# Attention and routed FFN on one core: a clear ahead of every indirect DMA, and another order and bank plan for the tile loop

## The reference, cut to what matters

```
x: (4, 1024, 256)      context: (4, 77, 256)
x = x + attention(layernorm(x), context)       # 16 heads of 16, softmax over 77 keys
n = layernorm(x)                               # without scale and shift
scores = sigmoid(n @ gate.T)                   # 32 experts
choose 4 of 8 groups by their best score + bias, then 6 experts in them
w = chosen scores / their sum * 2.5
x = x + sum over the 6 experts of w_e * down_e(silu(gate_e n) * up_e n)
      + shared_down(silu(shared_gate n) * shared_up n)
```

## Time and profile before

| | |
|---|---|
| median of 3 runs | 870.69 us (869.93 to 871.14) |
| profiled execution, its own time | 878.87 us |
| its span | 877.2 us, mean granted TensorE clock 0.896 |
| busy share of the span | PE 88%, DVE 57%, ACT 45%, POOL 59% |
| chain that ended last, by engine | PE 39%, POOL 31%, issue 17% |
| indirect DMAs on POOL | 192 scatters, mean 986 ns; 192 gathers, mean 1025 ns |
| pauses on POOL | 160, mean 615 ns |

### The profile page before, as it was taken

The page is one execution under the profiler, slowest core; times in us unless marked ns, Lnnn a source line. Parts: engine busy times, 40 slices in busy tenths (PEclk is TensorE's granted clock), DMA queues, the critical chain, the costliest instruction groups (busy, mean ns, idle before and its releaser), DMA issues.

```text
span 877.2 us, 17678 instructions
## 1 busy us (share of the span) xinstructions
PE 768.9 (88%) x5472; PEld 658.4 (75%) x5472; DVE 500.7 (57%) x1556; ACT 393.0 (45%) x822; POOL 517.3 (59%) x603
## 2 busy tenths in 40 slices
PE   4699989988899999959997999999999999899920
PEld 2488877777777777624655999999999998799920
DVE  4667666666666667522345223367666665466652
ACT  1264444444444444210111566666666665466610
POOL 0204777777777777777000000778888887888885
PEclk9698888899988888678999899999999999899965
DMA  9113444444444322245513355888888898788852
GB/s 292 42 46 112 132 133 139 138 137 138 139 141 153 120 84 90 103 152 196 188 49 96 110 172 165 239 249 267 262 269 264 258 268 250 209 247 261 257 156 72
DMA packets 120222, 149.01 MB, mean 170 GB/s; under 512 B 17265, under 2 KB 106741, under 8 KB 120002
## 3 DMA queue, kind: packets, MB, share of 16 engines
q1 hardware_dynamic: 99416, 94.33, 34.4%
q0 software_dynamic: 19200, 52.45, 19.9%
q10 hardware_dynamic: 1514, 1.09, 0.5%
HBM read 80.56 MB, written 67.26 MB: 169 GB/s over the span
## 4 chain that ended last, share of the span: by engine, by line
PE 39%; POOL 31%; issue 17%; SPq 4%; DVE 4%; DMA 4%; ACTq 1%; ACT 0%; POOLq 0%; DVEq 0%
POOL rows L480 19%; PE sc_ps L892 16%; PE bank L902 8%; PE sc_ps L787 6%; POOL hold L469 5%; PE sc_ps L876 4%; POOL work L513 3%; PE bank L798 3%; POOL rstd L487 2%; DMA work<-yrows,dest 2%; SPq L429 2%; SPq L423 1%; DVE stats L924 1%; DMA yrows<-work 1%; DMA wdn<-in_gate_b 1%
## 5 line engine op out<-in xcount | busy, mean ns | idle before, releaser
L513 POOL DMA_INDIRECT work<-yrows,dest x192 | 196.8, 1025 | 59.5 <-issue 26.8
L892 PE MATMUL sc_ps<-work 128*128 128x128 f32 x1792 | 222.4, 278 | 3.6 <-DVE work L1332 3.6
L480 POOL DMA_INDIRECT rows<-work,dest x192 | 189.4, 986 | 57.5 <-issue 47.7
L892 PEld LDWEIGHTS sc_ps<-work 128*128 128x128 f32 x1792 | 212.9, 195 | 4.0 <-issue 3.8
L469 POOL TENSOR_TENSOR hold<-cst 128x1 f32<-128x1 f32 x160 | 98.3, 615 | 138.7 <-DMA yrows<-work 134.5
L902 PE MATMUL bank<-wdn,work 128*128 x448 | 117.1, 384 | 7.6 <-DVE work L1287 7.6
L1313 DVE SCALAR_TENSOR_TENSOR work<-work 128x256 f32<-128x256 f32 x160 | 77.3, 483 | 57.2 <-DMA work<-yrows,dest 49.9
L1287 DVE TENSOR_TENSOR work<-work,sc_ps 128x256 f32<-128x256 f32 x112 | 46.9, 419 | 103.0 <-ACT work L613 80.0
L635 ACT ACTIVATE work<-bank 128x512 f32<-128x512 f32 x112 | 66.8, 596 | 52.7 <-PE bank L902 34.5
L902 PEld LDWEIGHTS bank<-wdn,work 128*128 128x128 f32 x448 | 77.1, 192 | 15.2 <-issue 9.3
L613 ACT ACTIVATE work<-sc_ps 128x256 f32<-128x256 f32 x112 | 42.9, 383 | 77.7 <-PE sc_ps L892 70.2
(11 more groups left out here) (163 smaller groups left out, 1098.1 us busy)
## 6 DMA issues: line engine op xcount, KB each, us to landing
work<-rows SPq DMA_DIRECT2D x224, 128.0 KB
yrows<-work SPq DMA_DIRECT2D x224, 128.0 KB
wgu<-in_egu SPq DMA_DIRECT2D x16, 512.0 KB
store<-in_x SPq DMA_DIRECT2D x8, 512.0 KB, 10.1
x1d<-work SPq DMA_DIRECT2D x32, 128.0 KB
wdn<-in_edn SPq DMA_DIRECT2D x8, 512.0 KB
work<-x1d SPq DMA_DIRECT2D x8, 512.0 KB, 3.7
out<-work SPq DMA_DIRECT2D x32, 128.0 KB
```

The costliest lines, as they stand in the source:

```text
L480: pool.indirect_dma_start(rows[:, :], bass.IndirectOffsetOnAxis(ap=dest[:, t, k:k + 1], axis=0), rowb[:, m, :], None).then_inc(scat[m], 16)
L513: pool.indirect_dma_start(yg[:, g % RG, :], None, yrows[0:n * P, :], bass.IndirectOffsetOnAxis(ap=dest[:, t, k:k + 1], axis=0)).then_inc(l ...
L892: last = mm(ps8[2 + m % 2][:, (2 * w + g) * P:(2 * w + g + 1) * P], wst[w][m % 2][:, k * 2 * I + g * I:k * 2 * I + (g + 1) * I], xeT[:, m ...
```

## The change

It has two parts. The first is POOL's pause: a memset of a 128x128 tile takes the place of the `pow`, it stands ahead of each of the 384 indirect DMAs, and what waits for a memset's semaphore is the next memset, not the DMA. The second part is the order of stages on all four engines, the plan of `bank[0..3]`, and the waits that follow from it. On POOL the second half of a tile's scatters comes one step later, so that between `inverse_std` of tile `t` and that of `t+1` now stand the scatters of tile `t-3` (before, of tile `t-2`). What is computed does not change.

```diff
-        hold = sb("hold", [P, 1])
+        hold = sb("hold", [P, P])
...
-        q_ps = bank[1][:, 0:D]
-        pT_ps = [bank[3], bank[2], bank[0]]
-        pv_ps = bank[3][:, 0:H * PV]
+        q_ps = bank[2][:, 0:D]
+        pT_ps = [bank[3], bank[3], bank[2]]
+        pv_ps = bank[0][:, 0:H * PV]
         oT_ps = bank[0][:, 0:D]
-        y_ps = bank[0][:, 0:D]
+        y_ps = bank[1][:, 0:D]
         x2T_ps = bank[2][:, 0:D].rearrange("p (k n) -> p k n", k=KT)
-        lg_ps = bank[2][:, 0:E]
-        rk_ps = bank[1][:, 0:E]
+        lg_ps = bank[1][:, 0:E]
+        rk_ps = bank[0][:, 0:E]
...
-            pauses = itertools.count(1)
+            pauses = itertools.count()
             def pause():
-                pool.tensor_tensor(hold[:, :], const("ones")[:, 0:1], const("half_neg")[:, 0:1],
-                                   ALU.pow).then_inc(S_["pause"], 1)
-                pool.wait_ge(S_["pause"], next(pauses))
+                done = next(pauses)
+                if done:
+                    pool.wait_ge(S_["pause"], done)
+                pool.memset(hold[:, :], 0.0).then_inc(S_["pause"], 1)
...
-                    pause()
                     for k in range(half * TOPK // 2, (half + 1) * TOPK // 2):
+                        pause()
                         pool.indirect_dma_start(rows[:, :], bass.IndirectOffsetOnAxis(ap=dest[:, t, k:k + 1], axis=0),
                                                 rowb[:, m, :], None).then_inc(scat[m], 16)
...
             def step(tile):
+                at_tile(tile, 4, scatter(1))
+                at_tile(tile, 0, inverse_std)
                 at_tile(tile, 3, scatter(0))
-                at_tile(tile, 3, scatter(1))
-                at_tile(tile, 0, inverse_std)
...
-                    if g % 2 == 0:
-                        pause()
+                    pause()
                     pool.indirect_dma_start(yg[:, g % RG, :], None, yrows[0:n * P, :],
```

Before, PE had (4 gate) (0 qk) (-1 tr_x) (2 tr_o) (1 tr_p0) (1 tr_p1) (-1 q_proj) (2 o_proj) (3 tr_x2) (1 pv0) (1 pv1) (1 pv2) (4 rank) (0 tr_p2) (3 s_early). Of PE's waits for banks, these are the ones that the text comes to:

```diff
             def rank(t, m, s):
                 need(pe, "sel", t)
                 need(pe, "selcum", t)
-                read_out(pe, "qT", t, 5)
-                if t >= 27:
+                read_out(pe, "oT", t, 3)
+                if t >= 29:
                     read_out(pe, "place", t, -1)
...
             def tr_x(t, m, s):
                 need(pe, "xn", t)
-                read_out(pe, "place", t, -6)
-                if 1 <= t <= 5:
-                    read_out(pe, "qT", t, -1)
+                read_out(pe, "x1", t, -4)
+                if 1 <= t <= 3:
+                    read_out(pe, "xnT", t, -1)
```

More of the change, by code:

```diff
@@ L583, in step @@
             def step(tile):
[L584 to L587, removed]
-                at_tile(tile, -1, norm1)
[L589 to L593, removed]
+                at_tile(tile, 3, ev_pT(2))
+                at_tile(tile, 4, ev_oT)
+                at_tile(tile, 6, gate_exp)
+                at_tile(tile, 3, ev_pT(0))
+                at_tile(tile, 1, ev_q)
+                at_tile(tile, 3, ev_pT(1))
+                at_tile(tile, 0, ev_xT)
+                at_tile(tile, 2, exps)
+                at_tile(tile, 5, ev_x2T)
+                at_tile(tile, -1, norm1)
             over_tiles(step)
@@ L686, in q_proj @@
                 need(pe, "xnT", t)
-                read_out(pe, "xnT", t, 0)
+                read_out(pe, "pT2", t, -2)
+                if 1 <= t <= 1:
+                    read_out(pe, "qT", t, -1)
                 for h in range(2):
@@ L729, in stage @@
                     if f == 0:
-                        read_out(pe, "pT0", t, 0)
+                        read_out(pe, "place", t, -4)
+                        if 1 <= t <= 3:
+                            read_out(pe, "oT", t, -1)
                     for c in range(4 * f, min(4 * f + 4, NCH)):
@@ L739, in tr_o @@
                 need(pe, "o", t)
[L740 to L742 removed]
+                read_out(pe, "o", t, 0)
                 for k in range(KT):
@@ L748, in o_proj @@
                 need(pe, "oT", t)
-                read_out(pe, "oT", t, 0)
+                read_out(pe, "gate_exp", t, -2)
+                if t <= 1:
+                    read_out(pe, "xnT", t, 3)
                 for k in range(KT):
@@ L764, in gate @@
                 need(pe, "xn2T", t)
-                read_out(pe, "xn2T", t, 0)
+                read_out(pe, "xnT", t, 5)
+                if t >= 27:
+                    read_out(pe, "x1", t, 1)
+                if t >= 31:
+                    read_out(pe, "gate_exp", t, -1)
                 for k in range(KT):
@@ L812, in step @@
             def step(tile):
+                at_tile(tile, -1, tr_x)
+                at_tile(tile, 2, pv(1))
+                at_tile(tile, 2, pv(2))
+                at_tile(tile, 0, qk)
+                at_tile(tile, 1, tr_p(2))
+                at_tile(tile, 1, tr_p(0))
+                at_tile(tile, 2, tr_o)
                 at_tile(tile, 4, gate)
-                at_tile(tile, 0, qk)
-                at_tile(tile, -1, tr_x)
-                at_tile(tile, 2, tr_o)
-                at_tile(tile, 1, tr_p(0))
+                at_tile(tile, -1, q_proj)
+                at_tile(tile, 5, rank)
+                at_tile(tile, 2, o_proj)
                 at_tile(tile, 1, tr_p(1))
-                at_tile(tile, -1, q_proj)
-                at_tile(tile, 2, o_proj)
                 at_tile(tile, 3, tr_x2)
                 at_tile(tile, 1, pv(0))
-                at_tile(tile, 1, pv(1))
-                at_tile(tile, 1, pv(2))
-                at_tile(tile, 4, rank)
-                at_tile(tile, 0, tr_p(2))
                 at_tile(tile, 3, s_early)
@@ L1133, in step @@
             def step(tile):
+                at_tile(tile, 5, group_top)
+                at_tile(tile, 3, x1_mean_var)
+                at_tile(tile, 5, group_take)
+                at_tile(tile, 3, x1_var_eps)
+                at_tile(tile, 2, inverse_sums)
+                at_tile(tile, 5, mask_groups)
+                at_tile(tile, 2, normalise)
+                at_tile(tile, 5, expert_top)
                 at_tile(tile, 5, expert_take)
-                at_tile(tile, 6, count_on)
-                at_tile(tile, 1, row_max(1))
-                at_tile(tile, 1, shift(1))
                 at_tile(tile, 5, expert_select)
-                at_tile(tile, 3, residual)
-                at_tile(tile, 3, x1_stats)
+                at_tile(tile, 0, row_max(0))
+                at_tile(tile, 3, norm2)
+                at_tile(tile, 0, row_max(1))
+                at_tile(tile, 4, gate_add)
+                at_tile(tile, 0, shift(0))
                 at_tile(tile, 5, chosen_scores)
                 at_tile(tile, 5, place_chosen)
-                at_tile(tile, 2, inverse_sums)
-                at_tile(tile, 2, normalise)
-                at_tile(tile, 3, x1_mean_var)
-                at_tile(tile, 4, gate_add)
-                at_tile(tile, 3, x1_var_eps)
-                at_tile(tile, 5, place_index)
-                at_tile(tile, 4, sigmoid)
-                at_tile(tile, 3, norm2)
-                at_tile(tile, 4, corrected)
-                at_tile(tile, 0, row_max(0))
-                at_tile(tile, 4, group_max)
-                at_tile(tile, 0, shift(0))
-                at_tile(tile, 4, group_top)
-                at_tile(tile, 4, group_take)
-                at_tile(tile, 4, mask_groups)
-                at_tile(tile, 4, expert_top)
+                at_tile(tile, 4, sigmoid)
+                at_tile(tile, 4, corrected)
+                at_tile(tile, 5, count_on)
+                at_tile(tile, 0, shift(1))
+                at_tile(tile, 2, residual)
+                at_tile(tile, 4, group_max)
+                at_tile(tile, 5, place_index)
+                at_tile(tile, 2, x1_stats)
             over_tiles(step)
```

21 lines of the change are left out of this document (9 added, 12 removed).

## The result

The changed kernel took 946.72 us (median of 4 runs, 942.6 to 956.31) against 870.31 for the kernel before beside it (4 runs, 867.3 to 871.14): ratio 1.09, 95% interval 1.0814 to 1.0987. The forecast was 841 us. Further down the same changed kernel takes 805.48 us in another set of runs, 0.942 of the kernel before. Both numbers stand, and most of what follows is about the difference.

A forecast was written before the change was run, and what follows sets the result against it. It took POOL, PE and the DVE loop as nearly level in the tile loop, and POOL's gather rate as the bound at the end. Tile loop -8 and gathers with tail -22 us took 870.7 to 841 us, range 826 to 856.

The forecast's parts named there:

- PE's 8.3 us: Expert stage, 714 to 843 us: PE's idle time before the change, forecast to go along with DVE's waits for gathered rows.
- the 3.88 us on DVE: Tile loop: DVE's wait at `place_chosen` in every second tile, read as PE's late results and expected to stay.
- stalled loop: Rival: tile loop stalls on a scatter's landing or `rank`'s late result, tile 11 us, total about 874 us; chance 0.06.
- costly clear: Rival: each clear ahead of 384 indirect DMAs costs a full POOL instruction, 0.56 us, total about 965 us; chance 0.08.
- The price of a clear: POOL, ahead of each indirect DMA: a 128x128 memset costs 0.15 us on top of the 0.30 us gap; bounds nothing and 0.56.
- POOL's tile: Tile loop: POOL's work per tile becomes 9.5 us against 9.4 before, with bounds of 8.1 and 12.0 us.
- The tile loop: POOL's rate and new order: -8 us, bounds nothing and 24 us gained at PE's busy time; 1.79 us ahead of `rank` can go.
- The landing: Tile loop: `norm2` newly waits for the last scatter of tile t-4; costs nothing up to a landing 4.4 us after its end.
- The gathers freed: Expert stage: gathers at 1.53 to 1.55 us meet PE's 1.56, ending DVE's row waits; rival "not freed": about 860 us, chance 0.11.
- The tail: After the last block's store: POOL abreast, the last gathers start sooner, 15 + 0.6 us gained.
- DVE's copies against POOL: Expert stage, shared ports: if copies held every second clear for 0.421 us, a gather takes 1.70 us, total about 878 us.
- the rival at 821 us: Clear hidden in the 0.30 us gap, loop at PE's pace: loop -24 us, gathers -24 to -27; chance 0.16.

The follow-up runs named there:

- the fourth set: Kernel after unchanged 805.48 us; old order without pauses 827.03; kernel after with waited one-column clears 802.83, with only scatters' clears waited for 818.19; kernel before 855.02.
- the third set: New order with unwaited pow 819.6 us; kernel before without pauses 824.64; kernel after with three clears 957.71, with only scatters' clears waited for 819.74; kernel before 851.50.
- second set: Among others: kernel before with its pow not waited for, 865.2 us; kernel after with waited one-column clears, 989.05 us; kernel before 876 to 879 us.

## Why the prediction was wrong

**Which step failed.** "POOL then just keeps up. DVE's waits for rows go, and PE's 8.3 us with them." The first two happened. The third did not: from 714 to 843 us PE idles 17.5 us in the place of 8.3, and the expert stage got 58.4 us longer. The working took it that the only tie between POOL's indirect DMAs and the other engines is when the rows land, and put the tie through the signals at nothing. On the chip of the result there is one: while gathers follow each other at 1.34 us, PE's signals reach ACT and DVE up to 4.5 us late in the rows shown, and the ring PE, ACT, DVE has no slack for it. Before, the pow ahead of every second gather kept the mean distance at 1.62 us, and the stage ran at 3.20 us a pair. The sign of it was in the rows and was read as something else: "at clock 0.85 PE has little room, and its late results (the 3.88 us on DVE)". PE's result was not late, its signal was, by 211.27 - 208.72 = 2.55 us. None of the rivals had this mechanism; the two slower ones (stalled loop, costly clear) had its sign only.

**Where signals are not late, the steps can be judged one by one**, by the kernel after in the fourth set.
- *The price of a clear*, 0.15 us on top of the 0.30: it is 0.22 long, and 0.09 of it shows (gathers 1.34 us apart, 1.25 without a clear). The gap ahead of a DMA shrinks from 0.30 to 0.17, so not all of it was a part of the DMA's own start. This term was mis-sized, and on the safe side.
- *POOL's tile*, 9.5 us: 8.77 (timeline, one `inverse_std` to the next with no idle time), halfway to the 8.1 of the lower bound:

```profile
212.97 0.57 POOL L488 TENSOR_TENSOR rstd<-var,cst 128x1 f32<-128x1 f32 x1
...
221.74 0.57 POOL L488 TENSOR_TENSOR rstd<-var,cst 128x1 f32<-128x1 f32 x1
```

- *The tile loop*, -8 us for POOL's rate and the order together: the last `place` is at 348.4 against 388.8 in the earlier trace rows, 40 us, more than the 24 of the outer bound; part of that is the set and not the kernel, since the kernel before is itself 15 us faster there. PE was not the floor that its busy time made it. Over 22 tiles in the middle of the loop a tile took PE 9.29 us before and 8.57 there, with the clock of the stretch at 0.92 in the place of 0.85, so the same work came out shorter. Ahead of `rank`, the 1.79 us of the earlier trace rows are gone: PE waits there for an eviction 0.2 us in all.
- *The landing*, "costs nothing" up to 4.4 us: DVE waits 31.3 us in all ahead of `norm2` (20 times, at most 6.4), 1 us a tile. The Trainium skill, Perfetto Trace Analysis, section "DMA Instruction — SWDGE (GPSIMD)", says that such an instruction ends in the profile when its descriptors are made, not when the data have moved; this wait agrees.
- *The gathers freed*: 154.00 of 154 us of PE, DVE's wait for rows 4.8 us in all. *The tail*: the last gather starts 15.6 us after the last `hidden`, against 28.2 before, so 12.6 of the 15.6 forecast.
- *DVE's copies against POOL.* By SBUF — State Buffer, section "Who interferes with whom", in the Trainium skill, a DVE instruction in a mode that takes the shared ports, as a copy can be, and a GpSimd instruction exclude each other: whichever starts first keeps the ports for its whole instruction, and the other is blocked so long. In the expert stage of the fourth set's trace 27 of the 192 clears start while a copy runs, and 23 of these take 0.38 to 0.50 us; the four that do not start within 0.05 us of the copy's start or end. Of the other 165 none takes over 0.232. One of the 23:

```profile
611.33 0.50 DVE L1340 COPY work<-wgu 128x512 f32 x1
...
611.57 0.39 POOL L472 MEMSET hold<- 128x128 f32 x1
```

  So the trace agrees with the rule. But a clear seldom meets a copy, the median of all 384 is 0.219 us, and the stage keeps PE's pace: the price is nothing.

**The whole.** Clear hidden and loop faster was the rival at 821 us, 0.943 of 870.7; the fourth set gave 0.942. That rival was near in its mechanism too, with a clear that shows 0.09 us instead of nothing. About half of the gain there comes without the new order: 827.03 us without pauses in the old order (0.965), and 805.48 for the kernel after, another 0.974. The clears in the old order were not run in such a set. On the chip of the result, the likeliest case, its range and the sign were all wrong.

**What stays open.** What makes the signals late in one set and not in another, and why at 1.35 us the tile loop takes anything from 10.3 to 11.6 us a tile. That PE's signals are late only while POOL issues is shown by the records of the semaphores; how the issue holds them is not. No run took the data or the indices out of the gathers, and the third set shows that close issue alone is not enough. The best kernel depends on this: one-column clears in the new order gave 0.939 and 1.126, the kernel after 0.942 and 1.09. An unwaited pow at the old places gained where it ran, 0.985 in the old order (second set) and 0.960 in the new (third), but each ran in one kind of set only.

## What to carry to other kernels

Before a pause or a slow instruction on a DMA-issuing engine is taken out, look in the trace of before for waits of other engines that end on nothing known while that engine issues; such a wait can mean that signals come late while that engine issues, as here, and then a faster issue can cost more than it frees. Compare the end of the instruction that raises the semaphore with the start of the one that waits for it. Take a large result, good or bad, to a second chip before explaining it by the kernel: after eight runs here a theory of distances stood, and the next four, elsewhere, brought it down. And a gap between two instructions is not a fixed cost because it is always there: price a new instruction in it from nothing up to its full length.

## What the runs showed of the hardware that was not expected

- Indirect DMAs on POOL: 0.95 to 0.97 us long as a median with clears or nothing between, 1.25 to 1.27 us apart with nothing between, 1.34 to 1.36 with a 128x128 clear (0.22 us) between, 1.44 to 1.46 if each waits for its clear, 1.87 with three.
- One kernel, line for line the same, took 989.05 us beside a kernel before of 879.23, and 802.83 beside one of 855.02. The difference is 186 us for it and 24 for the kernel before.
- Where signals were late, PE's finished groups were acted on by ACT up to 4.5 us late (861.29 + 1.95 to 867.77), 0.95 us after the last gather of a burst had ended, while PE and POOL themselves ran on. The signals of ACT, DVE and POOL were not late in any trace.
- In the third and fourth set no signal of PE was over 0.3 us late, with gathers as close as 1.25 us and DMA engines busy 0.90 of the time.
